# A graph layer on one core: branch and tests moved into and behind the window loop, x loaded in pieces, narrower key columns

## What is computed

```python
msg = x[src] + edge_attr_128                       # 53125 x 128
neigh = segment_sum(msg, dst, num_segments=3125)
rst = (1.0 + eps) * x + neigh
h = rst @ W1 + b1                                  # 3125 x 256
h = (h - mean(h, 0)) * rsqrt(var(h, 0) + 1e-5) * gamma + beta
out = relu(h) @ W2 + b2
y = x + out;  y = (y - mean(y, -1)) / sqrt(var(y, -1) + 1e-5)
```

## Time and profile before

| | |
|---|---|
| profiled execution | 265.49 us, its span 263.7 us, mean granted clock 0.972 |
| PE busy | 240.7 us (91%) |
| DVE / ACT / POOL busy | 187.8 / 127.9 / 172.6 us |
| first window on PE | 16.90 us |
| last block, start and length | 224.83 us, 3.65 us |
| DMA | 38.11 MB, mean 145 GB/s |

### The profile page before, as it was taken

How to read it: one execution, slowest core, us unless ns; L and a number is a source line. 1 busy time by engine, 2 the same in 40 slices (tenths; PEclk the granted TensorE clock), 3 DMA queues, 4 the chain that set the end, 5 groups by cost and what they waited for, 6 DMA issues and landing times.

```text
span 263.7 us, 6841 instructions
## 1 busy us (share of the span) xinstructions
PE 240.7 (91%) x2205; PEld 201.5 (76%) x2205; DVE 187.8 (71%) x686; ACT 127.9 (48%) x225; POOL 172.6 (65%) x113
## 2 busy tenths in 40 slices
PE   0649689999999999999999999999999999999980
PEld 0548568889999998788888888878888879845980
DVE  2978894768789986887887878777666511288882
ACT  0406512445565665455645555544444232176794
POOL 3058888888888888888888888888888600270000
PEclk9999956999999999999999999999999999999996
DMA  5975655677789888777888787877776400000034
GB/s 156 271 232 109 138 115 100 151 153 177 192 193 209 189 196 193 171 184 189 200 186 187 183 193 176 192 165 176 156 160 155 81 0 2 4 0 0 2 114 130
DMA packets 48957, 38.11 MB, mean 145 GB/s; under 512 B 5019, under 2 KB 47947, under 8 KB 48921
## 3 DMA queue, kind: packets, MB, share of 16 engines
q1 hardware_dynamic: 32829, 30.62, 40.3%
q0 software_dynamic: 14400, 6.56, 20.8%
q10 hardware_dynamic: 1692, 0.48, 1.0%
HBM read 36.05 MB, written 1.60 MB: 143 GB/s over the span
## 4 chain that ended last, share of the span: by engine, by line
PE 79%; DVE 12%; issue 3%; ACT 2%; DVEq 2%; DMA 1%; ACTq 1%
PE ps L682 28%; PE ps L690 20%; PE ps L720 9%; PE ps L714 7%; PE ps L636 4%; PE ps L781 3%; PE ps L706 2%; DVE hit_k L952 2%; PE ps L770 2%; DVE hit_k L949 2%; DVE aggT L1022 2%; PE ps L711 1%; ACT big L561 1%; DMA x_room<-in_dst_dram 1%; PE ps L619 1%
## 5 line engine op out<-in xcount | busy, mean ns | idle before, releaser
L438 POOL DMA_INDIRECT egat<-in_x_dram,srci x100 | 163.6, 1636 | 43.1 <-issue 28.3
L524 ACT ACTIVATE big<-ps 128x500 f32 x158 | 96.7, 612 | 109.8 <-PE ps L720 83.6
L690 PEld LDWEIGHTS ps<-hit_c,ebuf 128*128 128x128 f32 x632 | 103.2, 195 | 14.9 <-DVE hit_c L920 4.7
L690 PE MATMUL ps<-hit_c,ebuf 128*128 128x20 f32 x632 | 97.3, 232 | 6.4 <-DVE hit_c L920 4.6
L1022 DVE TENSOR_TENSOR aggT<-aggT,ps 128x20 f32 x208 | 35.9, 173 | 54.9 <-PE ps L690 35.5
L682 PE MATMUL ps<-big,xN 128*128 128x114 f16 (+8 forms) x225 | 59.7, 278 | 0.4 <-ACT big L524 0.3
L682 PE MATMUL ps<-big,x_room 128*128 128x114 f16 (+8 forms) x225 | 59.6, 278 | 0.0
L682 PE MATMUL ps<-big,xr 128*128 128x114 f16 (+8 forms) x225 | 59.5, 278 | 0.0
L720 PE MATMUL ps<-hit_k,hit_l 128*128 128x400 f16 x158 | 53.2, 337 | 0.0
L714 PE MATMUL ps<-hit_k,hit_l 128*128 128x300 f16 x158 | 46.5, 294 | 0.0
L952 DVE TENSOR_TENSOR hit_k<-iota_k,key 128x800 f16<-128x800 f16 x79 | 44.9, 568 | 0.0
(11 more groups left out here) (105 smaller groups left out, 209.3 us busy)
## 6 DMA issues: line engine op xcount, KB each, us to landing
ebuf<-in_edge_attr_dram SPq DMA_DIRECT2D x79, 256.0 KB
egat<-in_edge_attr_dram SPq DMA_DIRECT2D x49, 128.0 KB
egat<-in_x_dram,srci POOLq DMA_INDIRECT x100
out_dram<-big SPq DMA_DIRECT2D x5, 256.0 KB
w_sb<-in_L_gnn_W_dram ACTq DMA_DIRECT2D x2, 128.0 KB, 6.9
out_dram<-big SPq DMA_DIRECT2D x2, 128.0 KB
x_room<-in_dst_dram SPq DMA_DIRECT2D x1, 192.0 KB
x_room<-in_src_dram ACTq DMA_DIRECT2D x1, 192.0 KB
```

The source lines that it names most:

```text
L438: return nc.gpsimd.indirect_dma_start(to, None, x[:, :], bass.IndirectOffsetOnAxis(ap=ix, axis=0), compute_op=op)
L524: nc.scalar.activation(cnt[:, :, bass.ds(lows[m % LOADS], WIN)], ps[:, m % BANKS_C, 0:KEYS].rearrange("p (t n) -> p t n", n=WIN), ACT.Copy ...
L690: last = nc.tensor.matmul(ps[:, SUMS + w % BANKS_S, 0:WIN], rows_v[:, j * D:(j + 1) * D], hits_v, start=(j == 0), stop=(j == ROWS - 1))
```

## The change

- The tests leave the place ahead of the loop. DVE makes them in windows 85 (`find_bounds`), 88 (`find_worst`, and the memset of the end of `cnt`, which stood at window 14) and 94 (the flag); PE shares the result in window 91. The branches come late: on DVE and ACT behind the loop, on PE between two groups of preloads, on POOL behind its last work, on SP behind its loads. The fast path is now always computed; the general path redoes everything if the flag asks for it.
- `firsts` is clamped (two DVE instructions, limits from two iotas on POOL), so that the columns stay in range whatever the input; DVE waits for `firsts` ahead of the first `hits_k`.
- ACT instead of DVE copies rel, the gathered sources and carry out of PSUM; the turns have another order (rel, keys, lo, sources, b2, carry). The weights' five DMAs go from ACT's queue to the end of SP's first loads.
- x comes in seven pieces, each with its own semaphore, between the first chunks and slots.
- Key columns of the second row: 375 (FROM_B 5, WIN_B 15) instead of 400, made as 376; the idle matmuls have 375 too.
- Eight blocks instead of nine (the last takes 10 groups instead of 8 and 2), MARGIN 30 instead of 36, and the planner's order follows: gathered windows begin 6, 9, 11, 14, 18, 22, 26, 30 (before: 6, 9, 12, 14, 18, 22, 26, 30).
- `part_3` of pieces 3 to 6 is made by POOL, one behind each of the slots 1 to 4.

The diff, cut to its core:

```diff
-FROM_B = 4
-WIN_B = WIN - FROM_B
+FROM_B = 5
+WIN_B = 15
-BLOCKS_C = (10, 12, 17, 25, 31, 31, 22, 8, 2)
+BLOCKS_C = (10, 12, 17, 25, 31, 31, 22, 10)
-MARGIN = 36
+MARGIN = 30
+POOL_FROM = 3
...
+        TEST_F = 3
+        W_BOUNDS = READY[TEST_F] + 2
+        W_TESTS = W_BOUNDS + 3
+        W_WORST = W_TESTS + 3
+        W_SHARED = W_WORST + 3
...  SP
-            sp.dma_start(xN[:, 0:NT - 1, :], x_main).then_inc(x_loaded, 16)
+            chunk(0)
+            x_piece(X_ORDER[0])
+            slot(0)
+            x_piece(X_ORDER[1])
+            chunk(1)
+            x_piece(X_ORDER[2])
+            slot(1)
...
+            chunk(3)
+            x_piece(X_ORDER[6])
+            for n in range(3, SLOTS):
                 slot(n)
...  POOL
-            pool.wait_ge(path_known, 1)
-            flag = pool.value_load(wide[0:1, 0:1], min_val=0, max_val=1)
+            pool.wait_ge(sources_made, 1)
+            for n in range(NG):
+                k = n % SLOTS
+                pool.wait_ge(slot_loaded[k], 16 * (n // SLOTS) + 16)
+                for j in range(ROWS):
+                    m = n * ROWS + j
+                    gather(egat[:, k, j * D:(j + 1) * D], srci[:, m:m + 1], ALU.add).then_inc(slot_gathered[k], 16)
+                b = POOL_FROM + n - 1
+                if n > 0 and b < NB:
+                    t0, t1 = pieces(b)
+                    v = xr[:, t0:t1, :]
+                    pool.wait_ge(x_rest_made, b + 1)
+                    nc.gpsimd.tensor_tensor(x3[:, t0:t1, :], v, upper(v), ALU.subtract).then_inc(x_last_pool, 1)
...  PE
+                    if u == 0 and f == TEST_F + 1:
+                        pe.wait_ge(path_known, 1)
...
+                if w == W_WORST:
+                    pe.wait_ge(worst_found, 2)
+                    pe.wait_ge(block_added, TEST_F)
+                    nc.tensor.matmul(ps[:, ACC + (TEST_F + 1) % 2, 0:1], ones[0:Q, :], over[:, TESTS + 1:TESTS + 2],
+                                     start=True, stop=True).then_inc(worst_shared, 1)
...
+            pe.wait_ge(x_b2_added, 1)
+            preload(0, 4)
             pe.wait_ge(path_known, 1)
             flag = pe.value_load(wide[0:1, 0:1], min_val=0, max_val=1)
+            with pe.If(flag == 0):
+                pe.wait_ge(hidden_stored, NB * HH)
+                preload(4, len(ROW_PIECES))
+                products()
...  DVE
+            dve.wait_ge(rel_made, 1)
+            hits_c(0)
+            dve.wait_ge(firsts_loaded, 32)
+            dve.wait_ge(constants_made, 10)
+            nc.vector.tensor_tensor(firsts[:, :], firsts[:, :], least_first[:, 0:G], ALU.max).then_inc(lows_made, 1)
+            dve.wait_ge(lows_made, 1)
+            nc.vector.tensor_tensor(firsts[:, :], firsts[:, :], most_first[:, 0:G], ALU.min).then_inc(lows_made, 1)
...
+            dve.wait_ge(lo_made, 1)
+            hits_k(0)
+            dve.wait_ge(carry_made, 1)
+            hits_n(0)
+            hits_k(2)
...
                 if w % SPREAD == 1 and w // SPREAD < NB:
                     rest(w // SPREAD)
-                    part_3(w // SPREAD)
+                    if w // SPREAD < POOL_FROM:
+                        part_3(w // SPREAD)
+                if w == W_BOUNDS:
+                    find_bounds()
+                if w == W_TESTS:
+                    find_worst()
...
+                    nc.vector.memset(cnt[:, :, CNT - SPARE:CNT], 0.0).then_inc(spare_zeroed, 1)
...
+            dve.wait_ge(path_known, 1)
             flag = dve.value_load(wide[0:1, 0:1], min_val=0, max_val=1)
+            with dve.If(flag == 0):
+                last_sums()
+                hidden_stats(hidden_stored)
+            with dve.Else():
...
```

More of the change, by code:

```diff
@@ L344, in gnn_layer @@
         X_TILES = [(i, t) for i, b in enumerate(X_ORDER) for t in range(*pieces(b))]
+        TEST_F = 3
[3 more added lines that the diff above has]
+        W_SHARED = W_WORST + 3
+        assert W_SHARED + 2 < READY[TEST_F + 1] and sum(w in C_OF for w in range(W_SHARED)) < CORNER
         @block.sync
@@ L621, in turn_x, with hidden @@
                         last.then_inc(x_turned, 1)
+            def hidden(n0, n1, complete, made, stored):
+                for n in range(n0, n1):
+                    b, h = n // HH, n % HH
+                    pe.wait_ge(complete, b + 1)
+                    if n >= BANKS_C:
+                        pe.wait_ge(stored, n - BANKS_C + 1)
+                    nc.tensor.matmul(ps[:, n % BANKS_C, 0:width(b)], w1_sb[:, h * P:(h + 1) * P],
+                                     aggT[:, b * BANK:b * BANK + width(b)], start=True,
+                                     stop=True).then_inc(made, 1)
```

850 lines of the change are left out of this document (453 added, 397 removed).

## The result

The kernel after takes 270.96 us (median of 4 executions, 270.85 to 271.33), the kernel before, on the same chip, 265.69 us (4 executions, 265.31 to 265.93): a ratio of 1.0202, 95% interval 1.0187 to 1.0218. The change makes the kernel 5.3 us slower. Predicted were 266.3 us, with a range up to 270.0, which the result passes by 1.0 us. Ratios are of executions without disturbance, so in the experiments they are not always the quotient of the medians.

The account below looks back on a forecast made before the run. DVE was taken to set the pace up to window 11, then mostly PE; -0.5 gathers, -1.9 columns, -0.4 blocks, +2.7 tests, +0.2 shared test, +0.5 branches gave +0.6: 266.3 us as a median, range 262.8 to 270.0.

Parts of the forecast that it names:

- the likelier of the two signs: Whole kernel: slower was given 0.45, faster by over 0.2% 0.38, within 0.2% 0.17.
- 375 columns: Key matmuls: 25 columns fewer save 0.0104 us each, 2.0 us, of which 0.1 is lost: -1.9 us.
- The gathers behind POOL's new work: Windows 11 to 22: slot 2's gathers wait behind piece 3's third part; -0.5 us at window 22, bounds -2.6 and +4.
- the step ahead of the loop: DVE before the loop: first key hits go from 15.32 to 11.6, 3.7 us earlier, bounds 2.5 and 4.7.
- x in pieces: under DVE, nothing: Loads of x: no cost, since piece 3, last in the queue, is not asked for before 25 us.
- Tests inside the loop: DVE's windows 85, 88 and 94: tests cost +2.7 us, bounds +1.0 and +3.4; shared test on PE +0.2.
- the clock's second fall: Rival, windows 84 to 91: PE idles, ten us at 1.2 GHz cost 5, total 271.3; chance 0.12.
- Blocks: Last two blocks become one of 218 columns, 7.0 us against 7.6, block 0 adds 0.2: -0.4 us.
- Late branches: Behind the loop: DVE's jump between hidden_stats and the bn_aggr is uncovered; +0.5 us, bounds 0 and 1.6.
- POOL's arithmetic: Rival: slow beside DVE, 3.3 us for each of three pieces, window 22 at +4, total 270.8; chance 0.14.
- The lead: Rival: clock stays up at 33.9, PE follows the gathers, window 22 is 2.0 us earlier, total 264.3; chance 0.25.
- The tests did not hide: Rival, tests hidden: DVE has slack in the loop, the 2.7 us vanish, total 263.6; chance 0.09.

Follow-up runs that it names:

- the combined kernel: Kernel after with four edits: tests at windows 18 to 27, all third parts on VectorE, SP waits for dst rows, 400 columns; 263.67 us, ratio 0.9956.
- the run with the pieces spread: The combined kernel with rest and third part of x's pieces every third window, not second, tests at windows 21, 23, 25, 27; 265.38 us, ratio 0.9886.

## Why the prediction was wrong

The direction was the likelier of the two signs and came true; the size was missed by 4.7 us (5.2 against the profiled execution). By its steps:

**375 columns: -1.9 forecast, +1.0 measured. This step failed.** It priced a matmul by its columns. That holds for the idle matmuls (0.158 us, 375 columns in one piece) and not for the key matmuls, which write 25 runs of 15 from column 5 and cost 0.171, more than 25 runs of 16 (0.168), and delay the matmul behind them. No row of before showed a matmul that writes runs of odd length, so the price had to be bounded from both sides; the forecast gave it as known. This is 2.9 us of the miss of 5.2.

**The gathers behind POOL's new work: -0.5 forecast at window 22, +1.0 measured.** The mechanism was right in each link: POOL idle until rest(3), its third part (1.04 us, forecast 1.5, bounds 1.1 to 3.3) ahead of slot 2's gathers, PE's wait in window 11 (5.01 us, forecast 4.5), the clock falling at 34.5 all the same. What was off is when rest(3) comes, 27.77 and not 25.9, and that is the step ahead of the loop: the first key hits at 13.56 instead of 11.6. "x in pieces: under DVE, nothing" was wrong there, by 1.4 to 1.6 us: the new first loads hold up the last of the dst indices. The clamps cost 0.75 us instead of 0.4. The forecast looked at what waits for x, and not at what shares the DMA engines with it. It also had DVE set the pace from window 0 to 11. That holds from window 6 on; ahead of it PE at 1.2 GHz does, which the printed clock of 1.00 hid, and most of the first window's lead of 3.95 us is spent there.

**Tests inside the loop: +2.9 forecast with the shared test, +3.5 measured.** The place was right (reductions behind the block addition and the register loads, PE's wait in window 87), and so was the shared test (0.2). But of the other 3.3 us only 1.5 are waiting, where 2.7 were forecast, and 1.8 are the clock's second fall, which the sum had at nothing and the rivals at 5. The two errors nearly cancel, so that this term came out within 0.6 us is in part luck.

**Blocks: -0.4.** The last block took 7.01 us, as interpolated. What is left of the 5.8 us when the other terms are taken off (1.0, 1.0, 3.5 and 0.7) is -0.4 as well; it was not measured by itself.

**Late branches: +0.5 forecast, +0.7 measured, at another place.** DVE's jump costs nothing: from the start of the hidden layer to that of its bn_aggr and on to the output products before and after keep the same distance within 0.1 us. The loss is SP's. Its store of piece 6 waits for DVE's last two instructions; DVE's and SP's timelines, after and before:

```profile
264.41 0.73 DVE L1258 TENSOR_SCALAR big<-ps,big 128x128 f32<-128x128 f32 x2
...
266.02 0.47 SPq L483 DMA_DIRECT2D out_dram<-big  x1
```

```profile
259.36 0.73 DVE L1113 TENSOR_SCALAR big<-ps,big 128x128 f32<-128x128 f32 x2
...
260.11 0.45 SPq L412 DMA_DIRECT2D out_dram<-big  x1
```

The store was issued 0.02 us behind DVE's end before and 0.88 us behind it after. That SP was held up there is shown, by what (its code for the general path now stands ahead of the stores) is not.

**The rivals.** The clock did fall once more (0.12), but for 3.4 us, which cost 1.8 and not 5. POOL's arithmetic was not slow beside DVE (0.14: 3.3 us each; it took 1.04 to 1.66): DVE was stopped by it, which no rival had. The lead was not kept, though in the run with third parts on VectorE and in the combined kernel it was: there window 22 comes at 45.81 and 46.75, against 50.32 in the kernel before. The tests did not hide.

**The chances.** The range ended at 270.0 since the clock's second fall and a fully slow POOL were left outside as single rivals. Three terms off in the same direction, by 2.9, 1.5 and 0.6 us, did what no single rival would.

## What to carry to other kernels

A matmul that writes PSUM in runs is priced by rows of its own form: here, 25 columns fewer cost more time because the runs became odd. An instruction given to another engine to relieve a full one is worth looking at three ways: what it waits for there, what is queued behind it there (here, the gathers), and whether it stops the engine that it was to relieve. Tests that nothing waits for belong where the engine that makes them has time to spare: the same instructions cost 3.5 us at windows 85 to 94, behind a block addition and register loads (6.3 in one profile of the combined kernel), and one wait of about half a microsecond at windows 18 to 27, with PE at 1.2 GHz there or at 2.4. And a clock of 1.00 on the page is to be checked against the distance of two like matmuls, ahead of the clock's first entry above all.

## What the runs showed of the hardware

- A matmul of 375 fp16 columns takes 0.158 us in one piece, 0.163 as runs of 15 from an even column, 0.171 as runs of 15 from an odd one; 350 columns take 0.147 in one piece and as runs of 14 alike.
- POOL's tensor_tensor on 512 elements took 1.04 to 1.66 us and stopped the 16-bit comparisons of DVE that it met: 0.42 became 1.78, 0.46 became 2.52 us; an fp32 one of 0.31 became 2.47.
- Loads of edges and x on SP's queue, issued right behind the index rows, made a column of 4-byte words on ScalarE's queue land 1.6 us later (7.17 against 5.57 us, and 5.76 when they wait).
- PE ran at 1.2 GHz from the first key matmuls up to the first entry of the clock: 18.4 to 25.5 us in eleven of the fourteen profiles, 43.6 to 46.7 in the other three. The page prints 1.00 there; only the distance of like matmuls shows it (0.33 against 0.168 us for the key matmul of the kernel before, 0.293 against 0.168 for the idle matmul in the run with the pieces spread). Two profiles with the same code up to window 85 reach window 22 at 46.75 and, with the late rise, at 50.31.
- 3.4 us at 1.2 GHz in the middle of the loop cost 1.8 us, and 6.8 us some 2.9 to 3.5 (windows 87 to 100 against those of the run with tests at windows 18 to 27 or of the combined kernel, less the shared test and the wait in window 90): with PE busy throughout, about half of the stretch.
